# Head means of the query and key weights: a DVE reduction against halving additions on POOL

## What is computed

```
x = x + tanh(g_xattn[0]) * attention(layernorm(x), ctx, Wq, Wk, Wv)      # the front
x = x + tanh(g_ffn[0])   * ternary_ffn(layernorm(x), gate, up, down)     # the front
x = x + tanh(g_xattn[1]) * grouped_attention(layernorm(x), ctx, ...)     # behind it
x = x + tanh(g_ffn[1])   * experts(layernorm(x), ...)

# in grouped_attention, heads of d = 128:
q = _ln(_fp8_linear_pertensor(ln_out, wq, wq_scale, q_in_scale).reshape(b, s, g, hpg, d), qln_w, qln_b)
k = _ln(_fp8_linear_pertensor(ln_out, wk, wk_scale, k_in_scale).reshape(b, s, g, d), kln_w, kln_b)
# _ln subtracts the mean over the 128 outputs of a head, then divides by the deviation
```

## Time and profile before

| | us |
|---|---|
| three runs | 595.9, 596.17, 598.89 |
| median of them | 596.17 |
| the profiled execution | 595.5 |
| its span in the trace | 593.8 |
| front: from 0 to the barrier's release | 134.7 |
| PE busy, whole span | 554.6 (93%) |
| DVE busy, whole span | 469.5 (79%) |
| ACT busy, whole span | 379.6 (64%) |
| POOL busy, whole span | 366.6 (62%) |

### The profile page before, as it was taken

The page is one execution under the profiler, slowest core; times in us unless marked ns, Lnnn a source line. Parts: engine busy times, 40 slices in busy tenths (PEclk is TensorE's granted clock), DMA queues, the critical chain, the costliest instruction groups (busy, mean ns, idle before and its releaser), DMA issues.

```text
span 593.8 us, 11742 instructions
## 1 busy us (share of the span) xinstructions
PE 554.6 (93%) x4250; PEld 442.7 (75%) x4250; DVE 469.5 (79%) x972; ACT 379.6 (64%) x797; POOL 366.6 (62%) x299
## 2 busy tenths in 40 slices
PE   1998998969979999999989999999999999999996
PEld 0555444735658888888878788888888888888885
DVE  5399999787889999999999899999997754433433
ACT  1468778767876877777777877778764245343231
POOL 4031384204679878888789878787777527755231
PEclk9999999998989999999999999999999999999999
DMA  7793222115542041131482322223301001310002
GB/s 215 254 324 137 89 89 88 72 54 162 176 134 65 2 143 36 30 115 36 170 293 91 121 76 56 72 76 87 90 19 54 2 1 53 107 37 1 1 1 71
DMA packets 44569, 54.94 MB, mean 93 GB/s; under 512 B 8416, under 2 KB 30816, under 8 KB 44512
## 3 DMA queue, kind: packets, MB, share of 16 engines
q1 hardware_dynamic: 44512, 54.20, 27.9%
HBM read 41.60 MB, written 12.58 MB: 91 GB/s over the span
## 4 chain that ended last, share of the span: by engine, by line
PE 66%; DVE 4%; POOL 2%; issue 2%; ACT 1%; DVEq 0%; POOLq 0%
PE g_proj L2257 14%; PE g_proj L2345 10%; PE g_turn L2287 6%; PE g_op L2326 5%; PE g_scores L2300 5%; PE g_op L2265 3%; PE g_op L474 2%; PE g_op L475 2%; PE g_op L476 2%; PE g_proj L459 2%; PE g_proj L461 2%; PE g_proj L460 2%; PE g_turn L2309 2%; PE g_turn L459 1%; PE g_scores L459 1%
## 5 line engine op out<-in xcount | busy, mean ns | idle before, releaser
L1635 POOL TENSOR_TENSOR g_rs<-g_ve,neg_half 128x4 f32<-128x4 f32 x80 | 86.6, 1092 | 33.5 <-ACT g_ve L2007 32.6
L1656 POOL TENSOR_TENSOR g_cat<-g_yb,g_kb 128x1024 fp32r<-128x1024 bf16 x32 | 70.9, 2224 | 24.7 <-DVE g_yb L1819 24.7
L2257 PE MATMUL g_proj<-w_hi,g_xqc 128*128 128x512 f32 x192 | 84.8, 441 | 0.1
L503 POOL TENSOR_TENSOR m_h_lo<-m_h,m_h_hi 128x512 fp32r<-128x512 f32 x32 | 41.5, 1295 | 57.8 <-ACT m_h_hi L490 57.8
L2257 PE MATMUL g_proj<-w_lo,g_xqc 128*128 128x512 f32 x192 | 76.2, 397 | 0.0
L2033 ACT ACTIVATE g_qn<-g_proj,g_rs 128x128 f32<-128x128 f32 x192 | 54.9, 372 | 22.7 <-POOL g_rs L1635 12.6
L1763 DVE BATCH_NORM_STATS2 g_stats<-g_proj 128x6 f32<-128x256 f32 x160 | 60.3, 419 | 8.9 <-PE g_proj L2257 7.7
L2287 PE MATMUL g_turn<-ident,g_qn 128*128 128x128 f32 x384 | 57.4, 278 | 6.1 <-ACT g_qn L2033 6.1
L2287 PEld LDWEIGHTS g_turn<-ident,g_qn 128*128 128x128 f32 x384 | 44.2, 141 | 13.1 <-ACT g_qn L2033 6.7
L490 ACT ACTIVATE m_h_hi<-m_h 128x512 fp32r<-128x512 f32 x32 | 20.3, 633 | 49.2 <-DVE m_h L497 49.2
L1323 PE MATMUL f_bank<-f_w_ctx,f_ctxT 128*128 128x512 f32 x96 | 44.1, 592 | 0.0
(11 more groups left out here) (242 smaller groups left out, 1638.5 us busy)
## 6 DMA issues: line engine op xcount, KB each, us to landing
kvx_rows<-f_kept SPq DMA_DIRECT2D x24, 256.0 KB, 2.4
g_ksq<-kvx_rows SPq DMA_DIRECT2D x8, 512.0 KB, 4.6
g_kraw<-kvx_rows SPq DMA_DIRECT2D x16, 256.0 KB, 3.2
g_v<-kvx_rows SPq DMA_DIRECT2D x8, 512.0 KB, 4.1
m_raw<-in_L_W SPq DMA_DIRECT2D x16, 256.0 KB, 3.3
c_raw<-in_L_wqT SPq DMA_DIRECT2D x4, 512.0 KB, 5.7
f_w_ctx<-in_L_wkvxT SPq DMA_DIRECT2D x4, 512.0 KB, 7.3
c_praw<-in_L_wprojT SPq DMA_DIRECT2D x4, 512.0 KB, 5.5
```

Of the source, the lines that this page charges most:

```text
L1635: G.tensor_tensor(rs[:, at % NORMS, :], ve[:, at % NORMS, :], k["half"][:, 0:4], ALU.pow).then_inc(q["rs_done"], 1)
L1656: G.tensor_tensor(cat[:, h].rearrange("p h (b s) -> p b h s", b=2), yb[:, h, :].rearrange("p (b h s) -> p b h s", b=2, s=SEQ), kb[:, h, :] ...
L2257: last = T.matmul(bank(n, i)[:], xqc[:, n % 2, view * KT + c_, :], w[:, c_, :], start=c_ == 0 and part == 0, stop=c_ == KT - 1 and part == 1)
```

## The change

`weights.mean` leaves DVE's list in all six places. In its place POOL's list has `weights.mean_beside`: seven additions that halve a group of 128 columns down to one (64, 32, 16, 8, 4, 2, 1 left), each behind a wait for the one before, and the scaling by 1/128. The intermediate sums lie in a new buffer `tree` of 128 x 8 x 64. The same function is not used for the two context chunks: `context_mean` stays on DVE. The lists of POOL, DVE, ACT and PE are in another order; SP's is unchanged.

```diff
+    def mean_beside(self, pool, n, tree):
+        G, s, last = self.nc.gpsimd, self.sums[:, n, :], None
+        pool.wait_ge(self.loaded[n], 16)
+        of, at = self.raw[n][:].rearrange("p c (h d) -> p (c h) d", d=D), 0
+        for half in (64, 32, 16, 8, 4, 2, 1):
+            to = tree[:, :, 0:half] if half > 1 else s.rearrange("p (h o) -> p h o", o=1)
+            if half < 64:
+                pool.wait_ge(self.tree_done, self.centred_count(n) * 6 - 6 + at)
+            last = G.tensor_tensor(to, of[:, :, 0:half], of[:, :, half:2 * half], ALU.add)
+            if half > 1:
+                last.then_inc(self.tree_done, 1)
+            of, at = tree, at + 1
+        last.then_inc(self.sum_done, 1)
+        pool.wait_ge(self.sum_done, self.centred_count(n))
+        G.tensor_scalar(s, s, 1.0 / D, None, ALU.mult).then_inc(self.mean_done, 1)
...
+        tree = sb("tree", [P, 8, D // 2])
...
+            weights.mean_beside(pool, 0, tree)
             weights.centre(pool, 0)
+            ln.on_pool(pool, 1)
+            weights.mean_beside(pool, 1, tree)
             weights.centre(pool, 1)
-            ln.on_pool(pool, 1)
...
-            weights.mean(dve, 2)
             keep_values(0)
             divide(0)
             add_attention(0)
             ln.moments(dve, 2)
+            context_mean(0)
```

More of the change, by code:

```diff
@@ L136, in semaphores @@
         self.sum_done, self.mean_done, self.centred = take(f"{L}_wsum_done"), take(f"{L}_wmean_done"), take(f"{L}_centred")
-        self.hi_done, self.lo_done = take(f"{L}_hi_done"), take(f"{L}_lo_done")
+        self.hi_done, self.lo_done, self.tree_done = take(f"{L}_hi_done"), take(f"{L}_lo_done"), take(f"{L}_tree_done")
     def centred_count(self, n):
@@ L779, in _ @@
             weigh(0, 0)
+            weights.mean_beside(pool, 5, tree)
             weigh(0, 1)
             weigh(0, 2)
+            weights.centre(pool, 4)
             weigh(0, 3)
-            weights.centre(pool, 4)
             weigh(1, 0)
@@ L940, in _ @@
             ln.apply(dve, 2, lambda j: xn[:, 0, j, :])
-            weights.mean(dve, 3)
             largest(0)
             tern.means(dve)
-            context_mean(0)
             token_scales(0)
             less_max(1)
-            tern.clip(dve, 0)
-            round_tokens(0)
             keep_values(1)
             divide(1)
+            round_tokens(0)
             add_attention(1)
+            tern.clip(dve, 0)
             tern.clip(dve, 1)
@@ L958, in _ @@
             largest(1)
+            token_scales(1)
             hidden(0, 1)
-            token_scales(1)
             round_tokens(1)
+            product_scales(1)
             hidden(0, 2)
-            product_scales(1)
+            context_mean(1)
             hidden(0, 3)
-            weights.mean(dve, 4)
             hidden(0, 4)
+            tern.clip(dve, 2)
             weights.low(dve, 1)
             hidden(0, 5)
-            context_mean(1)
             hidden(0, 6)
@@ L976, in _ @@
             hidden(1, 1)
+            hidden(1, 2)
+            hidden(1, 3)
             mean_square(0)
-            hidden(1, 2)
-            weights.mean(dve, 5)
-            hidden(1, 3)
+            hidden(1, 4)
+            dve.wait_ge(q['ln_loaded'], 96)
+            V.reciprocal(inv[:], ins[:]).then_inc(q['ins_done'], 1)
             hidden_largest(0, 2)
-            hidden(1, 4)
             hidden_largest(0, 3)
+            hidden(1, 5)
             weights.low(dve, 2)
-            hidden(1, 5)
-            hidden(1, 6)
             hidden_scales(0)
@@ L1349, in _ @@
             turn_probs(1)
+            attend(1)
             turn_integers(0)
-            attend(1)
             context(0)
             context(1)
+            context(2)
             gate_up(0, 0)
-            context(2)
+            gate_up(0, 1)
             context(3)
-            gate_up(0, 1)
             context(4)
             gate_up(0, 2)
+            context(5)
+            turn_integers(1)
             gate_up(0, 3)
-            context(5)
             gate_up(0, 4)
-            turn_integers(1)
+            context(6)
+            context(7)
             gate_up(0, 5)
-            context(6)
             gate_up(0, 6)
-            context(7)
+            context(8)
             gate_up(0, 7)
-            context(8)
             gate_up(1, 0)
@@ L1373, in _ @@
             gate_up(1, 2)
+            gate_up(1, 3)
             context(10)
-            gate_up(1, 3)
-            context(11)
             gate_up(1, 4)
             gate_up(1, 5)
+            context(11)
+            gate_up(1, 6)
             context(12)
-            gate_up(1, 6)
             context(13)
@@ L1387, in _ @@
             context(EARLY)
+            down(0, 0)
             context(17)
-            context(18)
-            down(0, 0)
             turn_hidden(0, 2)
@@ L1393, in _ @@
             turn_hidden(0, 3)
+            context(18)
             down(0, 2)
```

91 lines of the change are left out of this document (45 added, 46 removed).

## The result

| | before | after |
|---|---|---|
| runs beside each other | 20 | 20 |
| median, us | 596.76 | 599.51 |
| lowest and highest, us | 595.67 and 599.09 | 596.62 and 601.95 |
| the profiled execution, us | 595.5 | 599.93 |
| its granted TensorE clock, mean | 0.990 | 0.982 |

The ratio is 1.0042, with a 95% interval of 1.003 to 1.0055. By the bound of 0.5% this is no change, but the kernel did become slower by some 2.5 us, since the interval leaves out 1. The two profiled executions differ by 4.4 us, more than the medians (2.75): that of before, at 595.5, is quicker than all 20 of its runs beside the changed kernel.

The account below looks back on a forecast made before the run. PE was taken to set the pace, busy 93% of 593.8 us. A later middle, +2.8 us, less 2.3 given back by DVE's relief made +0.5: 596.0 profiled, 596.7 us as median; range 593.2 to 601.0.

## What to carry to other kernels

Work handed from DVE to an idle POOL isn't free for DVE: list DVE's two-input and fast single-input instructions that will stand ready while POOL runs, and charge each the rest of POOL's instruction. Here the trees' own lockouts, 2.9 us, used up a saving of 2.8, and in an order not made for them the same trees cost 8.7 us. Place POOL's long instructions beside DVE's reductions and its work on PSUM, and don't count POOL's total. Where a change opens waits on PE in front of dense work, here 1.59 and 1.18 us, add a lower clock behind them to the sum (1.7 us here), and count the clock over many runs, not in one trace.

## What was not expected of the hardware

- A DVE scaling of 4 or 8 columns is held for all of what is left of a POOL instruction: 0.17 us became 1.22, 0.23 became 1.46, and three of 2 columns together 3.89.
- Four queued DVE scalings and POOL's additions take turns: 1.38 us of work takes 3.07 to 3.10 in all nine traces where the two met, and 4.58 and 4.81 us beside a centring or two. It goes both ways: five additions of 2.28 us took 4.12 where DVE was dense.
- POOL's smallest additions cost 0.20 us, no more, and waiting for its own last result 0.08 us.
- With 23 transposes that nobody reads, 8 of 12 runs had a mean clock of 0.990 or more; of the changed kernel 3 of 20, and 2 of 10 of its variant with the second tree early, run beside the same runs of before.
